# The masked expert weights of a mixture layer: one wide product on VectorE, and their sums on ScalarE

## What is computed

```python
h = hidden_states.reshape(T, H)
logits = (h @ router_w.T + router_b).reshape(T, O, E)
probs = jax.nn.softmax(logits.astype(jnp.float32), axis=-1)
w, sel = jax.lax.top_k(probs, TOP_K)
w = w / jnp.sum(w, axis=-1, keepdims=True)
c = jnp.zeros((T, E), dtype=h.dtype).at[t_idx, sel].add(w)
expert_out = jnp.einsum('th,eoh->teo', h, expert_w) + expert_b[None, :, :]
final = jnp.einsum('te,teo->to', c, expert_out)
```

## Time and profile before

| | |
|---|---|
| median of 3 runs | 1406.98 us (1406.31 to 1411.0) |
| profiled execution | 1404.72 us, its span 1403.0 us |
| TensorE busy | 1098.4 us (78%) |
| VectorE busy | 1117.2 us (80%) |
| ScalarE busy | 453.4 us (32%) |
| GpSimd busy | 271.3 us (19%) |
| granted TensorE clock, whole span | 0.922 |
| the mixture, from its first selection to its last weighing | 371.5 to 714.8 us |

### The profile page before, as it was taken

One profiled execution on the slowest core, in us unless ns is written; L12 is line 12 of the kernel. 1 busy time (PEld: TensorE's weight loads), 2 busy tenths in 40 slices (PEclk: granted clock), 3 DMA queues, 4 the chain that ended last, 5 costly groups with the idle time before them and its releaser, 6 DMA issues. The chain is left out here.

```text
span 1403.0 us, 19467 instructions
## 1 busy us (share of the span) xinstructions
PE 1098.4 (78%) x6516; PEld 580.4 (41%) x6576; DVE 1117.2 (80%) x2046; ACT 453.4 (32%) x708; POOL 271.3 (19%) x257
## 2 busy tenths in 40 slices
PE   0687878885587978878758888787877677999996
PEld 0243434443333434334323354363455344556564
DVE  7479696874389998999866888897899899677775
ACT  1044343432243242342314423404212133444443
POOL 7024241434224433234330000000000000000000
PEclk9699999998788989899869999998989899999999
DMA  3512121110000100101000000010010100000001
GB/s 90 120 51 67 54 57 63 46 32 24 14 0 0 39 0 0 37 0 38 0 15 1 1 18 15 1 31 0 7 23 14 26 27 12 1 1 0 0 1 60
DMA packets 36263, 34.66 MB, mean 25 GB/s; under 512 B 8024, under 2 KB 32856, under 8 KB 36192
## 3 DMA queue, kind: packets, MB, share of 16 engines
q1 hardware_dynamic: 36192, 33.75, 8.6%
HBM read 27.28 MB, written 6.29 MB: 24 GB/s over the span
## 5 line engine op out<-in xcount | busy, mean ns | idle before, releaser
L744 DVE TENSOR_REDUCE bm<-ps 128x4 f32<-128x512 f32 x160 | 104.6, 672 | 16.8 <-PE ps L541 15.5
L666 ACT ACTIVATE pt<-ps 128x1024 f32<-128x1024 f32 (+1 forms) x96 | 83.0, 881 | 98.7 <-PE ps L587 97.3
L920 POOL TENSOR_TENSOR wt<-lg,mid 128x2048 f32<-128x2048 f32 x16 | 75.3, 4709 | 185.4 <-DVE mid L1112 185.4
L537 PE MATMUL ps<-ks,qs 96*128 96x512 bf16 (+3 forms) x256 | 71.1, 324 | 44.6 <-DVE bm L744 28.0
L1034 ACT ACTIVATE wt<-wt 128x2048 f32<-128x2048 f32 x16 | 30.6, 1915 | 193.9 <-POOL wt L920 193.9
L1487 DVE TENSOR_TENSOR qk_lo<-ps,qk_hi 128x512 bf16<-128x512 f32 x80 | 54.9, 687 | 42.6 <-ACT qk_hi L1389 42.0
L815 POOL TENSOR_SCALAR rstd<-mv 128x4 f32<-128x4 f32 x12 | 2.7, 229 | 437.2 <-DVE mv L1496 217.1
L1656 PE MATMUL ps<-ew_hi,it_hi 128*128 128x256 bf16 x256 | 70.4, 275 | 17.1 <-DVE it_lo L1760 17.1
L1744 DVE SCALAR_TENSOR_TENSOR g<-g,ps 128x512 f32<-128x512 f32 x64 | 43.8, 685 | 46.0 <-ACT g L1694 45.7
L481 POOL TENSOR_SCALAR_AFFINE_SELECT pt<-pt 128x256 f32<-128x256 f32 (+1 forms) x96 | 46.8, 490 | 154.2 <-ACT pt L666 154.2
L1389 ACT ACTIVATE qk_hi<-ps 128x512 bf16<-128x512 f32 x80 | 47.7, 596 | 88.5 <-PE ps L1280 88.5
(11 more groups left out here) (228 smaller groups left out, 3003.9 us busy)
## 6 DMA issues: line engine op xcount, KB each, us to landing
qs<-scratch_q SPq DMA_DIRECT2D x64, 64.0 KB, 2.6
ks<-scratch_k SPq DMA_DIRECT2D x64, 64.0 KB, 2.6
q_next<-in_w_qkv SPq DMA_DIRECT2D x4, 768.0 KB, 4.6
X<-in_x SPq DMA_DIRECT2D x4, 512.0 KB, 7.0
w_next<-in_router_w SPq DMA_DIRECT2D x4, 512.0 KB, 4.1
w_next<-in_expert_w SPq DMA_DIRECT2D x4, 512.0 KB, 5.1
p_next<-in_w_proj SPq DMA_DIRECT2D x4, 512.0 KB, 5.9
out<-X SPq DMA_DIRECT2D x4, 512.0 KB, 4.6
```

The costliest lines, as they stand in the source:

```text
L537: pe.matmul(ps[:, o + P * i:o + P * (i + w)], qs[0:SHIFT, h, P * j:P * (j + 1)], ks[0:SHIFT, h, P * k0:P * (k0 + w)], start=(i == 0), stop ...
L666: act.activation(pt[kt][:, heads[0]:heads[-1] + 1, :], src, ACT.Exp).then_inc(s_exp, 1)
L744: ins = dve.tensor_reduce(bm[:, 2 * g + i // 5, 4 * (i % 5):4 * (i % 5) + 4], src.rearrange("p (k q) -> p k q", k=4), AX_X, ALU.max)
L920: pool.tensor_tensor(wt[:, :, :], lg[t % 2][:, :, :], over_experts(mid), ALU.subtract).then_inc(s_mid, 1)
```

## The change

Before, the eight experts' masked weights were eight instructions of VectorE on 256 columns each, every one with an accumulator output that gave the sum over the outputs. Now one VectorE instruction makes all 2048 products, in place in `far`, without sums, and counts up the new semaphore `s_kept`. ScalarE waits for it behind the sigmoid and runs eight copies of 256 columns (`far` onto itself) with an accumulator output, which write the eight sums into `cw` and count up `s_cw`. GpSimd's `from_middle` waits for `s_kept` in place of `s_cw` (its tile `wt` is no longer read by the sums), and VectorE's `from_second` waits for `s_cw` of the block before, since ScalarE reads `far`.

```diff
@@ gpsimd, from_middle
                     if not isinstance(n, int) or n:
-                        wait_alone(pool, s_cw, E * n, passed_pool)
+                        wait_alone(pool, s_kept, n, passed_pool)
                     pool.tensor_tensor(wt[:, :, :], lg[t % 2][:, :, :], over_experts(mid), ALU.subtract).then_inc(s_mid, 1)
@@ scalar
+                def token_weights(n, t):
+
+                    act.wait_ge(s_kept, n + 1)
+                    for e in range(E):
+                        act.activation(far[:, e, :], far[:, e, :], ACT.Copy, accum_out=cw[t % 2][:, e:e + 1]
+                                       ).then_inc(s_cw, 1)
+
                 x_parts(0)
                 tile_high(0, 0, 0)
                 logits(0, 0)
                 sigmoids(0)
+                token_weights(0, 0)
...
                         if after:
                             sigmoids(n + 1)
+                            token_weights(n + 1, after[1])
                         if t == 0:
 
                             act.wait_ge(load_next, 32 * b + 32)
@@ vector
                 def from_second(n, t):
 
+                    reach(dve, s_cw, E * n)
                     dve.tensor_tensor(far[:, :, :], lg[t % 2][:, :, :], over_experts(m2), ALU.subtract).then_inc(s_far, 1)
 
                 def token_weights(n, t):
 
                     dve.wait_ge(s_far, n + 1)
                     dve.wait_ge(s_wt, n + 1)
-                    for e in range(E):
-                        dve.scalar_tensor_tensor(wt[:, e, :], far[:, e, :], 0.0, wt[:, e, :], ALU.is_ge, ALU.mult,
-                                                 accum_out=cw[t % 2][:, e:e + 1]).then_inc(s_cw, 1)
+                    dve.scalar_tensor_tensor(far[:, :, :], far[:, :, :], 0.0, wt[:, :, :], ALU.is_ge, ALU.mult
+                                             ).then_inc(s_kept, 1)
```

More of the change, by code:

```diff
@@ L859, in layer0_mixture @@
         s_mid, s_far, s_wt, s_cw = st.sem("from_middle"), st.sem("from_second"), st.sem("sigmoids"), st.sem("token_weights")
-        s_c, s_u = st.sem("summed"), st.sem("experts")
+        s_kept, s_c, s_u = st.sem("kept"), st.sem("summed"), st.sem("experts")
         s_abs, s_pert = st.sem("magnitudes"), st.sem("ties_broken")
```

## The result

The changed kernel takes 1496.55 us (median of 4 runs, 1494.38 to 1497.1), the kernel before 1407.37 us in the same comparison: 1.0626 times as long, 95% interval 1.0604 to 1.0648. The forecast was 1509.5 us, the range 1480 to 1540. The profiled execution took 1494.38 us with a span of 1492.7; by the profiles the change costs 89.7 us, where +102.5 was forecast.

The account below looks back on a forecast made before the run. VectorE was taken to bound the mixture stage and so the kernel. Added 193.5 us (product, GpSimd wait, logits chain, splits, last sums) less 91.0 removed gave +102.5 us: 1509.5 us on the median, range 1480 to 1540.

Parts of the forecast that it names:

- Cheap sums: Rival: ScalarE's accumulator adds nothing to the plain copy's step, 2.6 us a block, 1487 us in all; chance 0.17.
- Dear sums: Rival: each ScalarE copy with its read drains the engine twice, 6.4 us a block, 1548 us; chance 0.10.
- The rest of the stall: VectorE standing between product and next selection while ScalarE makes sums, magnitudes and logits: 8.35 us, behind blocks 0 to 14.
- half speed: Rival: VectorE's wide product takes 4.6 us, 37 us more in all, 1546 us; chance 0.03.
- The wait for GpSimd: First product behind `far` waits for GpSimd's line 907 in eight rounds; carried over to the wide product, 18.4 us.
- TensorE costs clock, not time: Claim that TensorE, standing longer each round, loses granted clock (well under 0.88 in the stage) but delays nothing.
- TensorE becomes the bound: Rival: TensorE's clock stays low all round, its products end some 1.7 us late per round, 1537 us; chance 0.07.
- VectorE's load alone decides: Rival: next logits are ready when the product ends, so VectorE's 12.6 us less work is gained, 1394 us; chance 0.02.

Follow-up runs that it names:

- the fourth run: The changed kernel with GpSimd's line 907 held back until that round's wide product is through: 1476.69 us, ratio 1.0485 to the kernel before.
- The first experiment: The changed kernel with ScalarE's eight sums moved behind the next block's magnitudes and logits: 1407.48 us, ratio 0.9989 to the kernel before.

## Why the prediction was right

- **The mechanism.** The step that decided was the place of the new wait in ScalarE's queue: the overlap of the next logits with the products becomes a chain. Every round waits, as forecast, and moving the sums behind the logits takes the whole loss away. Shown.
- **The cost of the sums** is the term that was mis-sized. I took 0.49 us each from a plain copy's step and the fixed share of an instruction, 4.0 us a block, between 2.6 and 4.7. Measured is 0.40 and 3.2. The read is an instruction of its own and costs 0.19 us, as supposed (0.18), but half of it is hidden as the ends of plain copies are. Sixteen times 0.8 us is 12.8 us, all of the difference between +102.5 and the +89.7 of the profiles. Both of *Cheap sums* and *Dear sums* fall.
- **The rest of the stall.** 7.55 us where 8.35 was forecast, the difference being the sums; 8.21 where statistics stand in front and the splits of lines 1062 and 1063 lie between; 6.25 with normalisation; 9.86 in the one round with the splits and no statistics. Without the first wait of the stage 126.5 - 12.9 = 113.6 us; forecast were 125.3 + 9.2 - 9.1 = 125.4, less 15 x 0.8 = 12.0.
- **The wide product**: 2.29 us undisturbed, 5.07 and 4.11 behind line 907; sixteen of them 55.0 us, and forecast were 36.6 + 18.4 = 55.0. The row of `far` was the right price, and *half speed* is excluded. The wait for GpSimd was inherited in full, and the fourth run shows that it is one.
- **The balance.** Added 55.0 + 113.6 + 3.4 us, removed 67.6 + 14.3: +90.1 against the stage's 89.3.
- **TensorE costs clock, not time.** The granted clock in the stage fell to 0.80, the tie-break products took 2.05 us (2.07 in the earlier trace rows), and ScalarE's magnitudes waited for no product of TensorE within the rounds. *TensorE becomes the bound* falls.
- **The other side.** *VectorE's load alone decides* was put at 1394, for the case that the logits are ready when the product ends. The first experiment built that case and gave 1407. The step that failed there is the price: 12.6 us off VectorE were counted as if VectorE bounded every round, though the prediction's own first section had nine waits for logits, 14.3 us of them after the start. The run's own expectation allowed for that, but not for the last block's sums, for line 912 and for the rounds in which ScalarE waits for TensorE, and it missed too. How much of the missing gain is the change's and how much is scatter of those rounds stays open.

## What to carry to other kernels

When work moves to an engine with much idle time, read first what stands behind it in that engine's queue and who waits for that; the 193.9 us for which ScalarE stood idle in front of its sigmoids were no room for sums that had to wait for VectorE ahead of VectorE's own next input. A wait added to an in-order queue should stand behind everything that does not need it. And before a busy engine's load is made lighter, subtract the rounds in which it already waits: there the gain only becomes waiting.

## What the runs showed of the hardware

- An accumulating copy of 128x256 on ScalarE is two instructions, 0.40 and 0.19 us, at a step of 0.40 us; without the accumulator the step of that copy is 0.31. On VectorE the accumulator of the same size is a read of 0.08 us and costs 0.01 in the step (0.35 with it in the kernel before, 0.34 in the run with narrow products).
- VectorE and GpSimd hold each other up by whole instructions, in both directions. Line 912 takes 0.67 us alone and 2.71 behind the wide product; line 907 takes 2.12 and 3.09 to 3.15 us in the gap, 4.18 and 5.14 behind `far`. The four instructions of a normalisation on VectorE, which read one tile of full width each and two values per partition, took 4.15 us in place of 1.37 when line 907 (546.04 to 549.19) began behind the first of them:

```profile
543.30 2.29 DVE L1134 SCALAR_TENSOR_TENSOR far<-far,wt 128x2048 f32<-128x2048 f32 x1
545.51 4.15 DVE L1082 TENSOR_SCALAR xn<-X,mv,rstd 128x256 f32 x4
553.12 1.22 DVE L1109 TENSOR_TENSOR h<-lg 128x1024 f32<-128x1024 f32 x1 [3.47 <-ACT lg L1029]
```

  That is the kernel with line 907 in the gap, where it cost nothing: the wait behind it is 3.47 us in place of 6.25. The Trainium skill, "SBUF — State Buffer", "SBUF: two separate sides", names both kinds: two SBUF inputs, or one input in a mode that uses both ports. The trace agrees for two inputs. For the normalisation it shows the wait (one of its four instructions lasts 3.18 us in place of 0.40) but not the mode.
- One long instruction in place of eight short ones holds the other engine up for longer: GpSimd's line 912 took at most 0.92 us beside the narrow products, and up to 2.72 beside the wide one, where it comes late enough to meet the selection.
